# Routed attention: GpSimd issues the gathers of a batch ahead of the scatter they stood behind

## What is computed

```python
scores_q, idx_q = route(x, q_routing_token, NQ)        # 128 query tokens of 512
scores_kv, idx_kv = route(x, kv_routing_token, NKV)    # 256 key and value tokens
routed_q = jnp.take_along_axis(x, idx_q[..., None], axis=1)
routed_kv = jnp.take_along_axis(x, idx_kv[..., None], axis=1)
routed_out = heavy_attn(routed_q, routed_kv, scores_kv, gamma_heavy, wq_heavy, wkv_heavy, wo_heavy)
routed_out = routed_out * scores_q[..., None]
heavy_out = jnp.zeros_like(x).at[jnp.arange(b)[:, None], idx_q].set(routed_out)
return light_out + heavy_out
```

## Time and profile before

| what | value |
|---|---|
| median of 3 runs | 3009.7 us |
| range of the runs | 3007.76 to 3009.99 us |
| the profiled execution | 3006.64 us |
| its span, first to last instruction | 3004.9 us |
| mean granted TensorE clock | 0.924 of full speed |
| TensorE (PE) busy | 2630.8 us, 88% |
| VectorE (DVE) busy | 2108.6 us, 70% |
| ScalarE (ACT) busy | 1824.4 us, 61% |
| GpSimd (POOL) busy | 1369.4 us, 46% |

### The profile page before, as it was taken

How to read it: one execution, slowest core, us unless ns; L and a number is a source line. 1 busy time by engine, 2 the same in 40 slices (tenths; PEclk the granted TensorE clock), 3 DMA queues, 4 the chain that set the end, 5 groups by cost and what they waited for, 6 DMA issues and landing times. The chain is left out here.

```text
span 3004.9 us, 66861 instructions
## 1 busy us (share of the span) xinstructions
PE 2630.8 (88%) x23534; PEld 1755.3 (58%) x23534; DVE 2108.6 (70%) x5817; ACT 1824.4 (61%) x3725; POOL 1369.4 (46%) x1544
## 2 busy tenths in 40 slices
PE   7999999888499999999799999988878479998794
PEld 4888887666133333333378888766665235555663
DVE  5888885555478998888378888645566357777563
ACT  3887665665156666666578766656653158876631
POOL 1223224243446776765422322433355565664446
PEclk9999998999579999999899999999978669999897
DMA  3100000111332333332000000011154456564343
GB/s 105 38 21 19 21 20 22 30 38 36 81 83 68 86 86 76 76 86 65 16 22 19 19 21 21 23 28 41 38 146 102 71 155 152 138 148 118 99 142 41
DMA packets 217570, 196.59 MB, mean 65 GB/s; under 512 B 48704, under 2 KB 194240, under 8 KB 216640
## 3 DMA queue, kind: packets, MB, share of 16 engines
q1 hardware_dynamic: 200240, 176.02, 22.8%
q0 software_dynamic: 16896, 16.27, 3.5%
q10 hardware_dynamic: 144, 0.52, 0.0%
HBM read 97.92 MB, written 93.74 MB: 64 GB/s over the span
## 5 line engine op out<-in xcount | busy, mean ns | idle before, releaser
L1880 DVE CUSTOM_DVE_ANT_0 la_ps<-la_ps,la_tri 128x512 f32<-128x512 f32 (+3 forms) x1024 | 482.2, 515 | 92.6 <-PE la_ps L1407 85.2
L1684 ACT ACTIVATE la_prob<-la_ps 128x512 f32<-128x512 f32 x640 | 373.8, 602 | 242.1 <-PE la_ps L1418 235.1
L1407 PE MATMUL la_ps<-la_ks,la_qs 48*128 48x512 bf16 (+3 forms) x1024 | 256.6, 319 | 44.4 <-DVE la_mx L1880 28.6
L477 POOL TENSOR_TENSOR f2l_prob<-f2l_prob,f2l_rec 128x512 f32<-128x512 f32 x128 | 130.5, 1040 | 319.7 <-DVE f2l_rec L699 319.7
L477 POOL TENSOR_TENSOR f1l_prob<-f1l_prob,f1l_rec 128x512 f32<-128x512 f32 x128 | 130.5, 1040 | 314.8 <-DVE f1l_rec L699 314.8
L1274 POOL TENSOR_SCALAR_AFFINE_SELECT la_prob<-la_prob 128x512 f32<-128x512 f32 x256 | 159.4, 634 | 210.9 <-ACT la_prob L1684 210.7
L1418 PE MATMUL la_ps<-la_qs,la_ks 50*128 50x512 bf16 (+3 forms) x1024 | 242.7, 309 | 6.0 <-issue 2.1
L1878 DVE TENSOR_REDUCE ca_mx<-ca_ps 128x4 f32<-128x512 f32 x256 | 174.2, 687 | 95.5 <-PE ca_ps L1407 94.7
L1418 PEld LDWEIGHTS la_ps<-la_qs,la_ks 50*128 50x128 bf16 x1024 | 67.2, 94 | 234.3 <-ACT la_prob L1684 161.9
L1684 ACT ACTIVATE ca_prob<-ca_ps 128x512 f32<-128x512 f32 x256 | 152.1, 602 | 81.9 <-PE ca_ps L1418 81.9
L1450 PE MATMUL la_ps_o<-la_prob,la_v 128*32 128x512 f32 (+3 forms) x2048 | 199.0, 462 | 0.0
(11 more groups left out here) (483 smaller groups left out, 7329.1 us busy)
## 6 DMA issues: line engine op xcount, KB each, us to landing
stack_image<-la_parts SPq DMA_DIRECT2D x192, 128.0 KB, 2.4
stack_image<-ca_parts SPq DMA_DIRECT2D x192, 128.0 KB, 2.4
la_qs<-stack_image SPq DMA_DIRECT2D x64, 192.0 KB, 3.4
la_ks<-stack_image SPq DMA_DIRECT2D x64, 192.0 KB, 4.3
ca_qs<-stack_image SPq DMA_DIRECT2D x64, 192.0 KB, 3.5
ca_ks<-stack_image SPq DMA_DIRECT2D x64, 192.0 KB, 4.4
light_rows<-f1l_xr SPq DMA_DIRECT2D x64, 64.0 KB, 1.5
light_out<-g_y SPq DMA_DIRECT2D x64, 64.0 KB, 1.6
```

Of the source, the lines that this page charges most:

```text
L477: nc.gpsimd.tensor_tensor(pr[:, g], pr[:, g], rc[:, g].rearrange("p (h o) -> p h o", o=1).broadcast_to([P, PAIRS, P]), ALU.mult).then_inc( ...
L1407: last = nc.tensor.matmul(bank[:, col:col + width], qs[u][rows, h // 2, qblk * P:(qblk + 1) * P], ks[u][rows, h // 2, keys], start=True, s ...
L1684: nc.scalar.activation(prob[q % 2][:, n], ps2[n % 2][:], ACT.Exp, scale=SM).then_inc(S["p_sb"], 1)
L1880: last = nc.vector.tensor_tensor_reduce(bank[:, col:col + width], bank[:, col:col + width], tri[:, T - width:T], 1.0, -BIG, ALU.add, ALU.m ...
```

## The change

In GpSimd's stream of `heavy_attention` the gathers of a batch are issued one step of the loop earlier. Step `i` issues the gathers of batch `i + 2` and then the scatter of batch `i - 1`, where it was the scatter of batch `i`. The waits of each gather and of each scatter are the same as before; the loop has one step more, and its first step has no scatter.

```diff
--- before.py
+++ after.py
@@ -786,10 +786,13 @@
 
         @block.gpsimd
         def _(pool):
-            for b in range(B):
-                if b + 2 < B:
-                    pool.wait_ge(S["xs_ps"], b + 1)
-                    gather_rows(nc, route, b + 2)
+            for i in range(B + 1):
+                if i + 2 < B:
+                    pool.wait_ge(S["xs_ps"], i + 1)
+                    gather_rows(nc, route, i + 2)
+                if i == 0:
+                    continue
+                b = i - 1
                 pool.wait_ge(S["f_sb"], b + 1)
                 nc.gpsimd.indirect_dma_start(out=route["out"][b][:, :], out_offset=bass.IndirectOffsetOnAxis(ap=index[:, 0, b:b + 1], axis=0),
                                              in_=routed[b % 2][:, :], in_offset=None, compute_op=ALU.add,
```

## The result

The changed kernel takes 2965.7 us (median of 4 runs, 2962.4 to 2973.3); the kernel before took 3009.8 us beside it (4 runs, 3007.8 to 3015.1). The ratio is 0.9864, 95% interval 0.9841 to 0.9887: 44 us less. The forecast was 2968.1 us, 41.6 us less. A second series, of 6 runs, gave 2971.0 us and a ratio of 0.9873 (0.9854 to 0.9892).

A forecast was written before the change was run, and what follows sets the result against it. A closed loop from transposes through output projection, `routed`, scatter and gathers was taken to bound heavy attention's rounds. Removing waits (38.5 us) and clock dips (3.1 us) saves 41.6 us: 3009.7 to 2968.1 us, range 2959 to 2979.

The forecast's parts named there:

- The loop: Heavy attention: a batch's gathers leave only after the scatter of the batch three before, giving rounds of 13.38 us.
- A free round: Heavy attention with no wait for gathers: 10.19 us from transposes to L873, then 1.97 us to the next transposes.
- The waits: TensorE's waits for gathers before 13 transposes per pass, with the overlap at L873: 38.5 us saved in both passes.
- dip: A heavy-attention round in which TensorE's granted clock falls to about 0.50 after a long wait, costing 1.02 us.
- The clock: Three slowed rounds behind waits of over 2.2 us in the first pass disappear: 3.1 us saved, bounds 0 and 3.1.
- The new place of the wait: GpSimd's wait on `xs_ps` before the earlier gathers is already met, so it costs nothing and delays no scatter.
- rival a: Waits for gathers go but clock slowdowns stay or come elsewhere: only 38.5 us saved, 2971.2 us; chance 0.13.
- The tail: End of each pass: VectorE's waits for the last read-backs, 12.2 us in all, remain in either order.
- rival d: Slower: later stages give the saving back through TensorE's clock, 3018 us; chance 0.01.
- (b): Another loop, nearest VectorE's normalisation before L805, becomes the bound: about 19 us saved, 2990 us; chance 0.03.
- (c): TensorE is held at L815 by something just before the gather: nothing measurable, 3010 us; chance 0.03.

The follow-up runs named there:

- the second trace of before: The kernel before, unchanged, traced once more: 3002.1 us in one run.
- the old order with a pause: The kernel before with one waited-for GpSimd memset of 128x2048 ahead of the gathers of batches 3 to 15: 3063.6 us, ratio 1.0143.
- the old order with the values first: The kernel before with TensorE's first matmul of the values moved ahead of the transposes of the probabilities: 3011.0 us, ratio 1.0003.
- two pauses: The changed kernel with two waited-for GpSimd memsets of 128x2048 ahead of the gathers of batches 4 to 15: 2971.6 us, ratio 0.9849.
- the gathers doubled: The changed kernel with the gathers of batches 4 to 15 issued twice, the second time into buffers nobody reads: 2973.6 us in one run.

## Why the prediction was right, point by point

- *The loop bounded the rounds.* Shown: with the loop closed a faster TensorE makes the rounds no shorter; taking the scatter out, or swapping it behind the gathers, opens the loop in the old order; a pause in it counts in full.
- *A free round is 10.19 + 1.97 = 12.16 us.* Exact, in both passes.
- *The waits are worth 19.5 and 19.0 us.* The second pass, without a dip in either trace, measures this term alone: 219.60 - 200.61 = 18.99 us.
- *The clock, 3.1 us in the first pass.* The first pass measured 23.1 us, 22.7 of them in its 13 rounds, against 22.6 forecast, so the sum for this pair of traces holds. But as a term for the kernel's time it was sized on one trace: the second trace of before has one dip where the first had three. Over the two traces it is 4 dips in 2 executions, some 2 us each time. That dips need the waits is well supported: no round between the first and the last of a pass dips in any of the seven traces where the transposes wait for nothing, and 16 of 26 rounds do in the old order with a pause, where a wait is 2.7 us on average. The length of the wait doesn't decide it alone: in the old order with the values first three of the four dips stand behind waits of 1.71 to 1.96 us, while waits of 2.88 and 2.63 us in the two traces of before have none behind them.
- *The new place of the wait costs nothing, no scatter is held up.* GpSimd idles 5.87 us before a scatter, the 5.9 that were forecast, for `routed` and not for `xs_ps`.
- *The dips would stay (rival a).* They didn't: the two traces of after have none between the second and the last transposes of either pass. The medians alone couldn't have told, since the rival's 2971.2 us lies 5.5 us from the first and 0.2 us from the second.
- *The tail stays.* VectorE's two waits for the last read-backs are 12.0 us in all (12.2 before).
- *No other stage gives it back (rival d).* The rest of the span was 4 us longer in this trace, inside the 12 us by which it varies from trace to trace. An effect of a few us there can't be excluded.
- *The rivals (b) and (c)* are refuted by the round of 12.16 us.

The median fell by 44.1 us in the first series and 37.9 in the second (3008.9 to 2971.0); 41.6 lies between. That the first median came within 3 us of the forecast is partly luck, as its interval alone allows a fall of 34 to 48 us; what confirms the forecast is the length of the rounds. The passes of the two pairs of traces differ by 42.0 and 38.3 us, and the rest is the spread of the other stages.

## What to carry to other kernels

When an engine waits for a load, follow the load's own queue back: if it stands behind an instruction that needs the result of the same round, the wait is part of a closed loop, and making anything outside the loop faster gains nothing until the load is moved. A round of the trace that had no such wait gives the new period before any change is made. After the move ask the bound again: here the next wait, on TensorE itself, was worth 18 us more, though the same edit had been worth nothing a step earlier.

## What the runs showed of the hardware that I had not expected

A memset on GpSimd holds VectorE's small TENSOR_SCALAR operations: 0.35 us became 1.56 beside memsets of 1.80 us. The Trainium skill, "SBUF — State Buffer", section "Who interferes with whom", has this as an exclusive lock, in which the one that comes first blocks the other for a whole instruction, where VectorE's instruction works in a mode that takes both ports (no run here shows whether these did). The rows agree with it for the memset. For an indirect DMA they agree in part: with two pauses VectorE was held to the end of the gather, with the gathers doubled it was not held at all.

The other way round, an indirect DMA on GpSimd becomes longer when a normalisation on VectorE is under way as it starts, and the extra goes to whichever stands there. It is the scatter's in the old order (2.52 us against 1.55 to 1.63 with none under way), and the gathers' where these come first (1.11 and 1.52 us against 0.94). A normalisation that starts behind it does nothing: with two pauses 12 scatters have one that starts 0.01 to 0.06 us behind them, and they take 1.61 to 1.63 us. Taking an instruction out of such a place saves less than its measured duration.

The price of a short wait on TensorE was more than the idle time that the profile shows before its matmuls: 0.56 us of start-to-start distance for 0.40 us of idle, and 0.07 us more than the idle time for each wait on a gather. The distance between the starts of two matmuls, with the wait and without it, gives the price; the idle time before the matmul and that before the weight load don't.
